# A graph network on one core: node features scaled chunk by chunk, and selections put ahead of one-hots

## What is computed

```python
def sage_conv(x, src, dst, Wl, bl, Wr):          # mean over the neighbours
    agg = segment_sum(x[src], dst) / maximum(cnt, 1.0)
    return agg @ Wl.T + bl + x @ Wr.T

h = relu(layernorm(x))
x = x + sage_conv(relu(sage_conv(relu(sage_conv(h)))))        # three layers
h = relu(layernorm(x))                                        # the factor of a node is its rstd
messages = gelu((h[src] + edge_attr) @ We1 + be1) @ We2 + be2
aggregated = segment_sum(messages, dst)
u = (1.0 + eps) * h + aggregated
x = x + gelu(u @ Wu1 + bu1) @ Wu2 + bu2
```

## Time and profile before

| | us |
|---|---|
| median of 3 runs | 973.55 (972.28 to 975.14) |
| the profiled execution, its own time | 975.46 |
| its span, first to last instruction | 973.5 |

### The profile page before, as it was taken

The page is one execution under the profiler, slowest core; times in us unless marked ns, Lnnn a source line. Parts: engine busy times, 40 slices in busy tenths (PEclk is TensorE's granted clock), DMA queues, the critical chain, the costliest instruction groups (busy, mean ns, idle before and its releaser), DMA issues.

```text
span 973.5 us, 22393 instructions
## 1 busy us (share of the span) xinstructions
PE 921.0 (95%) x8724; PEld 700.1 (72%) x8724; DVE 502.8 (52%) x1958; ACT 247.9 (25%) x434; POOL 379.3 (39%) x399
## 2 busy tenths in 40 slices
PE   2977999999899999999989999999999999999995
PEld 1734555555545455555679999999998999999994
DVE  6589999995211112112267555543644553644541
ACT  2576677773111011101111111111111111110211
POOL 2000000000000000211178777777777777777772
PEclk9969999999999999999979999999999999999997
DMA  4200011102000000000085434443543444543431
GB/s 135 65 2 12 3 14 13 12 14 65 1 1 1 1 1 1 22 11 12 13 172 158 128 100 133 122 129 95 152 118 96 137 130 108 147 110 106 127 99 32
DMA packets 46832, 68.00 MB, mean 70 GB/s; under 512 B 15268, under 2 KB 25477, under 8 KB 46594
## 3 DMA queue, kind: packets, MB, share of 16 engines
q1 hardware_dynamic: 35202, 42.90, 16.2%
q0 software_dynamic: 11520, 23.62, 9.4%
HBM read 63.18 MB, written 3.30 MB: 68 GB/s over the span
## 4 chain that ended last, share of the span: by engine, by line
PE 84%; DVE 11%; DMA 1%; ACT 1%; issue 1%; SPq 0%; ACTq 0%; DVEq 0%
PE f_ps L1174 25%; PE f_ps L1225 24%; PE f_ps L1279 11%; PE f_ps L1210 9%; DVE f_region L602 2%; DVE f_region L600 2%; PE f_ps L1059 2%; PE f_ps L1052 2%; DVE f_region L606 2%; DVE f_region L604 2%; PE f_ps L1149 2%; PE f_ps L1111 1%; DMA f_rcntT<-in_dst_pt 1%; PE f_ps L1070 1%; PE f_ps L1247 1%
## 5 line engine op out<-in xcount | busy, mean ns | idle before, releaser
L553 POOL DMA_INDIRECT f_adj<-table,f_table_idx x360 | 355.1, 986 | 110.1 <-issue 108.8
L1174 PE MATMUL f_ps<-f_adj,f_parts 125*128 125x500 fp8e4 (+1 forms) x1575 | 331.5, 352 | 0.1
L1225 PE MATMUL f_ps<-f_parts 125*128 125x128 bf16 x4200 | 250.9, 220 | 3.9 <-DVE f_parts L790 3.9
L1225 PEld LDWEIGHTS f_ps<-f_parts 125*128 125x128 bf16 x4200 | 244.3, 98 | 11.0 <-issue 8.6
L1174 PEld LDWEIGHTS f_ps<-f_adj,f_parts 125*128 125x128 bf16 x1575 | 143.6, 97 | 130.0 <-issue 11.1
L538 POOL TENSOR_TENSOR f_rest<-f_region,f_parts 125x512 f32<-125x512 f32 (+1 forms) x7 | 7.3, 1049 | 464.5 <-ACT f_parts L1017 464.5
L929 ACT CAST f_adj<-f_ps 128x500 f32 x213 | 125.9, 591 | 56.8 <-PE f_ps L1059 41.3
L1279 PE MATMUL f_ps<-f_adj 128*128 128x94 f32 (+20 forms) x984 | 128.0, 275 | 3.5 <-ACT f_adj L1039 3.5
L1279 PEld LDWEIGHTS f_ps<-f_adj 128*128 128x128 f32 x984 | 118.3, 192 | 6.0 <-issue 5.9
L770 DVE TENSOR_SCALAR f_adj<-f_iota,f_dst_abs 128x94 f32<-128x94 f16 (+4 forms) x416 | 87.4, 283 | 60.7 <-PE f_ps L1279 60.7
L1210 PE MATMUL f_ps<-f_We,f_region 128*128 128x128 f32 x832 | 115.0, 282 | 0.8 <-DVE f_region L704 0.8
(11 more groups left out here) (135 smaller groups left out, 481.4 us busy)
## 6 DMA issues: line engine op xcount, KB each, us to landing
f_region<-in_edge_attr_T SPq DMA_DIRECT2D x103, 256.0 KB
f_adj<-table,f_table_idx POOLq DMA_INDIRECT x360
f_parts<-in_src_row SPq DMA_DIRECT2D x14, 256.0 KB
f_adj<-inv SPq DMA_DIRECT2D x1, 1562.5 KB
table<-f_region SPq DMA_DIRECT2D x6, 250.0 KB
out<-f_xT SPq DMA_DIRECT2D x6, 250.0 KB, 2.6
f_rcntT<-inv SPq DMA_DIRECT2D x5, 250.0 KB, 3.8
f_xT<-in_xT SPq DMA_DIRECT2D x1, 812.5 KB, 6.3
```

The costliest lines, as they stand in the source:

```text
L553: pool.indirect_dma_start(out=rows[:, r % RW, j * D:(j + 1) * D], out_offset=None, in_=table, in_offset=bass.IndirectOffsetOnAxis(ap=table ...
L1174: ins = pe.matmul(ps[:, dense_ps(i):dense_ps(i) + width(c)], parts[0:NP, (l % 2) * 3 + p, b, :], adj[0:NP, b, lo:hi].bitcast(F8), start=b ...
L1225: ins = pe.matmul(z_ps(g, j), select[0:NP, u % SELECT, j * P:(j + 1) * P], parts[0:NP, 3 + p, b, :], start=b == 0 and j == 0 and p == 0, s ...
```

## The change

Five things are changed.

- SP writes, awaits and broadcasts `rstd` for every chunk right behind the chunk's table write, into `rcntT`, whose chunk `mean_rows` of the third layer has read by then. `rstdT` and its one large broadcast go.
- In the turn of the last chunk, and before its table write, SP waits for all 21 products and issues the source rows and the destination tiles.
- `node_scale` of chunks 0 to 4 moves into the dense part (each in the slot of the next chunk's rows), those of chunks 5 and 6 in front of the edge loop.
- The six small steps of `eps1` and `be2` move to slot 221, behind `check_repeats`.
- DVE makes the selections of group 0 first, then waits for the destination tiles and makes the one-hots; and PE's selections wait for `lowest3` chunk by chunk.

```diff
@@ Plan.__init__
                 self.put("split", o + 2, q)
+                if 0 < q < s.NC - 1:
+                    self.put("scale", o + 2, q - 1)
@@ fast_path
-        rstdT, o = carve(flat, o, (N,), F32)
@@ SP
             for c in range(NC):
                 b = s.blocks(c)
+                if c == NC - 1:
+                    sp.wait_ge(dense_done, LAYERS * NC)
+                    for i in range(2):
+                        sp.dma_start(src_rows[:, i, :], src_columns(i)).then_inc(src_in[i], 16)
+                    sp.dma_start(dst_tile[:, :], t["dst_tiles"]).then_inc(dst_tile_in, 16)
                 sp.wait_ge(rows_kept, c + 1)
                 sp.dma_start(table[b[0] * NP:(b[-1] + 1) * NP, :].rearrange("(b p) d -> p b d", p=NP),
                              grows[0:NP, c % 2, 0:len(b) * D].rearrange("p (b d) -> p b d", d=D)
                              ).then_inc(rows_out[c % 2], 16)
-            for i in range(2):
-                sp.dma_start(src_rows[:, i, :], src_columns(i)).then_inc(src_in[i], 16)
-            sp.dma_start(dst_tile[:, :], t["dst_tiles"]).then_inc(dst_tile_in, 16)
-            sp.dma_start(inv.rearrange("(b p) -> p b", p=NP), rstd[0:NP, :],
-                         allow_slow_non_contiguous=True).then_inc(rstd_out, 16)
-            sp.wait_ge(rstd_out, 16)
-            sp.dma_start(rstdT[:, :], inv.partition_broadcast(P)).then_inc(rstd_in, 16)
+                sp.wait_ge(agg_kept, 2 * NC + c + 1)
+                sp.dma_start(in_nodes(inv, c).rearrange("(b p) -> p b", p=NP), columns(rstd, c),
+                             allow_slow_non_contiguous=True).then_inc(rstd_out, 16)
+                sp.wait_ge(rstd_out, 16 * (c + 1))
+                sp.dma_start(at(rcntT, c), in_nodes(inv, c).partition_broadcast(P)).then_inc(rstd_in[c % 2], 16)
@@ DVE
+            def node_scale(c):
+                dve.wait_ge(rstd_in[c % 2], 16 * (c // 2 + 1))
+                dve.scalar_tensor_tensor(out=at(uT, c), in0=at(hT, c), scalar=col["eps1"][:, 0:1], in1=at(rcntT, c),
+                                         op0=ALU.mult, op1=ALU.mult).then_inc(h_scaled, 1)
+            def split_be2():
+                dve.wait_ge(small_in, 16 * 9)
...
                 if slot == CALM:
                     check_repeats()
-            dve.tensor_scalar(col["eps1"][:, :], col["eps1"][:, :], 1.0, None, ALU.add).then_inc(be2_ready, 1)
...
+                    split_be2()
+                for c in plan.due("scale", slot):
+                    node_scale(c)
...
-            dve.wait_ge(be2_ready, 6)
-            dve.wait_ge(small_in, 16 * 9)
+            for i, b in s.selections(0):
+                select_sources(i, b)
             dve.wait_ge(dst_tile_in, 16)
             dve.tensor_copy(dst_abs[:, :], dst_tile[:, :]).then_inc(abs_ready, 1)
             dve.wait_ge(abs_ready, 1)
             for g in range(OH_AHEAD):
                 window_onehots(g)
-            for i, b in s.selections(0):
-                select_sources(i, b)
+            for c in range(NC - 2, NC):
+                node_scale(c)
             for g in range(END):
                 if g == KEEP:
                     keep_flag()
-                if 3 <= g < 3 + NC:
-                    node_scale(g - 3)
@@ PE, take_sources
                     else:
-                        pe.wait_ge(lowest3, NC)
                         pe.wait_ge(rows_kept, NC)
+                if i == 0 and b % s.NBC == 0:
+                    pe.wait_ge(lowest3, b // s.NBC + 1)
                 pe.wait_ge(select_ready, u + 1)
```

27 lines of the change are left out of this document (12 added, 15 removed).

## The result

The changed kernel took 992.28 us (median of 4 runs, 991.5 to 994.24), the kernel before 974.35 (4 runs) beside it: a ratio of 1.019, with a 95% interval of 1.0171 to 1.0209. That is 17.9 us slower, where 9.4 had been forecast, and outside the range. The profiled execution took 991.5 us with a span of 989.6, 16.1 more than the 973.5 of before. The two executions differ by 2.15 us before anything that the change touches: PE's hole begins at 251.89 us instead of 254.05 (in rows 1, the start of L1146 less its 2.89). So 16.1 + 2.15 = 18.2 us are to be found behind that point, and they are found in four places. They are those of this pair of executions; against others the first one comes out smaller, as run 1 shows.

A forecast was written before the change was run, and what follows sets the result against it. PE works almost without a break and POOL's gathers finish level with it, so a late POOL reaches the end; 2.1 (hole) + 1.5 (clock) + 5.8 (POOL) = +9.4 on 973.55 gives 983.0 us, range 977.0 to 989.0.

The forecast's parts named there:

- the round trip of chunk 5: Passage to edge stage: SP waits for chunk 5's inv write, issued 485.8, landing 493.2, before issuing chunk 6's transfers.
- a later start of POOL reaches the end of the kernel unless POOL makes it up on the way: Edge stage: POOL starts 8.5 us late, regains 2.5, and the end is late by 5.8 us.
- the sign: End of run: last DVE add well over 2.8 us behind the last gather would mean PE, not POOL, ends it.
- PE's lateness: Passage to edge stage: PE is 4.2 us late, less than POOL's 5.8 beside it, and the larger counts.
- `node_scale` in front of `pre`: Before the edge loop: chunk 6's scaling waits for its round trip, ending at 506.4 beside gathered rows at 507.
- The split: At 254 us: the chain in slot 221 lengthens PE's hole by 2.1 us; a slow clock behind it adds 1.5.
- POOL catches up: Rival, 0.18: in the edge stage POOL regains all 4.9 us, clock stays up, PE's 4.2 at most counts; 976.7 to 979.9.
- Fast write: Rival, 0.08: chunk 5's four-byte write is answered as fast as the counts' writes, 1.5 us each; 975.7 to 977.2.
- early selections: Rival, 0.05: SP reaches the source rows by 487.2, PE loses its 3.93 us hole before the selections; 970.7.
- Longer still: Rival, 0.13: inv write behind the table takes 9 us or more, nothing regained, clock low for longer; +15.5, 989.0.
- The stalls of the first gathers: POOL's first 25 gathers: mean 1170 ns against 973 later, excess 4.9 us, beside L796; half, 2.5 us, taken as regained.
- the rule that I had set against this: Edge stage: by the Trainium skill selections and one-hots hold POOL, L796 would not matter, nothing returns; 2.5 us more.

The follow-up runs named there:

- run 1: Kernel before with only the six steps of eps1 and be2 moved to slot 221: 976.13 us against 974.62, ratio 1.0016.
- run 3: Kernel before with POOL held back some 5 us by five memsets in front of a gather at 851 us: 974.99 us, ratio 1.0012.
- run 5: Changed kernel with each chunk's rstd write ahead of its table write: ratio 1.0051 to the kernel before, total not read; passage 33.8 us.
- run 4: Changed kernel with node_scale of chunks 5 and 6 in groups 5 and 7 of the loop: 986.6 us, ratio 1.0132 to the kernel before.
- run 2: Changed kernel with the six split steps one slot earlier (220): 990.3 us, ratio 1.0172 to the kernel before.
- run 10: Run 7's kernel with the split at slot 220 and source rows and tiles before chunk 5's table write: 973.89 us, ratio 1.0011 to the kernel before.
- run 6: Changed kernel with one rstd write for the last two chunks, behind source rows, tiles and last table write: ratios 1.0002 and 1.0083, totals not read.
- run 7: Run 6's kernel with node_scale of chunks 5 and 6 in groups 5 and 7: ratios 0.9994, 1.0025 and 1.001 to the kernel before.
- run 9: Same kernel as run 10, on chips of the 1211 to 1218 us kind; with three repeats, ratios 1.0011, 0.9868, 1.0012 and 1.011.
- run 8: Kernel before with only early source rows and tiles, selections before one-hots, and PE's waits chunk by chunk: ratios 0.9996 and 0.9999.

## Why the prediction was wrong

The direction and the first cause were right: SP stands in the round trip of chunk 5 with chunk 6's transfers behind it. The size was wrong by 8.5 us, and the step that carried the sum was the wrong one.

- **The step that failed: "a later start of POOL reaches the end of the kernel unless POOL makes it up on the way".** POOL started 13.0 us late against the row addition (505.98 - 486.18 = 19.80, before 491.09 - 484.30 = 6.79), not 8.5. It made up 463.59 - 458.49 = 5.1 of it, more than the 2.5 taken, and run 3 shows 2.7 to 4.9 us of further room at the end. POOL's own path asks for 5.2 us or less. The path that counted was PE's, and I had set that at 4.2 and dropped it as the smaller. The level finish misled me: two engines that end together say nothing about which had room on the way. That PE stands still for 2.2 us in 445 says it. The prediction had named the sign, a last addition well over 2.8 us behind the last gather: it was 10.3.
- **PE's lateness, forecast at 4.2, was 12.6.** Three of its terms were too small. The round trip of chunk 5 took 9.4 us instead of 7.4: behind the table, 2.2 us by run 5, where I took 1.1, and 7.2 with nothing ahead, where I took 6.3 with its issue after the first layer's 6.04. The landings: POOL began 7.1 us after the last table write was issued, which had been 3.4; I had added 0.7 for 900 KB in the queues, and it was 3.7. The gathers of group 0 took 8.2 us from POOL's start in run 4, where I had 7.4 and the kernel before 10.5.
- **`node_scale` in front of `pre` was named and priced at nothing**, "beside it", since its round trip was to end 0.6 us before the gathered rows. Its 125 pieces, in busy queues, took 11.2 us (499.21 to 510.37) and the broadcast another 5.7, to 516.08; I had 6 and 3.8. Run 4 gives its price: 5.7 us of the whole, nearly 5 of them in the passage, and not in my sum.
- **The split: right in kind.** The hole cost 1.3 us, not 2.1: all six steps ran quick without POOL, not the two that I had singled out (1.35 us for the chain). The slow stretch was 2.7 us in this execution, in place of 1.5. Runs 1 and 2 put both together at 1.5 and 2.0 us by medians; the 3.6 of my sum was too high for the mean case.
- **The slow clock behind the passage (2.9 us) was missing.** I had charged the clock for the hole at 254 us and not for the two new ones, though the earlier trace rows showed it for this very place.
- **The rivals.** "POOL catches up" had the right engine at the end and the wrong number behind it, as it took the same 4.2 for PE. "Fast write" and "early selections" are out by the 9.4 us. "Longer still" had the right round trip, 9 us or more, and through POOL alone came to 989.0.
- **The stalls of the first gathers.** I tied them to L796 (in the change the L726 of `node_scale`) beside them. Their mean from POOL's start was 1170 ns before and, in groups by line for a like stretch, in the change and in run 10:

```profile
L558 POOL DMA_INDIRECT f_adj<-table,f_table_idx x29 | 27.9, 961 | 22.2 <-DMA table<-f_region 13.6 <-issue 8.5
```

```profile
L567 POOL DMA_INDIRECT f_adj<-table,f_table_idx x26 | 28.4, 1093 | 7.9 <-issue 7.9
```

Over like stretches with four full scalings the mean is 1170 (before), 1130 and 1148 (runs 1 and 3); with one it is 961 (the change), 1045 (run 2), 1136 (run 4) and 1093 (run 10). In run 2 five gathers take 1.2 to 1.9 us, and no scaling stands beside any of them. So a stall doesn't need L796; whether L796 adds to them isn't shown. As for the rule that I had set against this, by the Trainium skill (SBUF — State Buffer, "Who interferes with whom") the selections and one-hots of DVE would hold POOL, but in the change they stand in the same stretch (505 to 540) and no gather behind the first takes over 1.1 us. The same section lets an instruction with two inputs in SBUF, as L796 is, meet a GpSimd instruction that reads SBUF, so that L796 "would not matter" did not follow from it. What makes the stalls stays open.

With the terms as measured the sum would have been: hole and clock 1.5 to 4.0, PE's passage 12.6, the clock behind it 2.8, the end -1.2, together 15.7 to 18.2.

## What to carry to other kernels

Before a late engine is charged to the end of a run, look which engine stands still least over the whole stage: its start is the one that counts, and an engine beside it may have room even if both finish together. That room has an end, and it differs between executions (2.7 and 4.9 us here). A wait for a DMA's own round trip belongs behind everything that others wait for, on the issuing queue and on the engine that uses its result; and an early issue is worth nothing if its queue hasn't got there yet. Before work is drawn forward on an engine, ask what it meets at the next join: here the selections came 3 us sooner and stood 5.5 us in front of the sum.

## What the runs showed of the hardware

- **A write of four-byte pieces took 6 to 14.5 us to be confirmed**, from its issue: 500 pieces some 6 us in the first layer, 7.2 us with nothing ahead (run 5) and 9.4 behind 250 KB; 125 pieces 11.2 us with 1,030 KB issued in the 2.2 us ahead of them. 625 pieces took 11.3 to 13.1 us behind source rows and tiles (runs 6 and 7) and 8.1 to 9.1 where those had gone out earlier (runs 9 and 10); all 3125 took 11.1 in the kernel before and 13.8 and 14.5 in run 8. The waits of SP's queue in the change, over all chunks:

```profile
SPq L503 <- DMA inv<-f_rstd: 63.0, 7, 10.8
```

  Here the count of pieces mattered less than what was in the queues. The Trainium skill (DMA: Bandwidth & Descriptors, "Anatomy of one DMA — SWDGE (gpsimd) path") has a fixed cost of about 2 us for a DMA whatever its size, on the path that GpSimd issues. No write of this form, all issued by SP, came near it; the counts' writes in 500-byte pieces did, with waits of 1.5 us.
- **DVE's small steps on 128x128 took 0.20 to 0.29 us at 254 us**, with POOL idle. Beside POOL one of two casts of that size had 1.20 and the other 0.25.
- **The granted clock isn't the same in all executions at one place.** Behind a hole of 2.89 us it was 1.00 in the kernel before and 0.50 in run 10; over the twenty profiles a slow stretch followed that hole in six of ten and the hole of 4.2 us in ten of ten (run 1). One and the same kernel had both (run 9 and its repeats). A slow stretch seen, or not seen, in one profile is a possibility, not a price.
- **Chips differ by more than the change.** The same kernel takes 974 us on two chips and 1211 to 1218 on four, all of it from the first gathers on, with PE waiting for "issue" again and again. What makes them wait stays open.
